# Holding the second group's cell stores and some late weights back until the first group's batch 7 has been gathered

## What is computed

```
h      = leaky_relu(bn1(conv2d(x, stem_w, stride 4)))        # 96 channels, 24 x 24
offset = conv2d(h, off_w, stride 4)                          # 2 numbers for each of 16 taps, 6 x 6 tokens
h      = leaky_relu(bn2(deform_conv(h, offset, dcn_w)))      # bilinear samples, 192 channels, 36 tokens
h      = h + attention(layernorm(h))                         # 12 heads, exp features; W_qkv, W_proj, b_proj, gamma, beta
h      = h + ffn(layernorm(h))                               # 3 experts W1, W2 chosen per image
```

## Time and profile before

| | us |
|---|---|
| median of 3 runs | 433.98 |
| lowest, highest | 433.89, 437.59 |
| the profiled execution | 433.47 |
| its span in the trace | 431.7 |
| PE busy | 375.2 |
| DVE busy | 291.9 |
| ACT busy | 218.0 |
| POOL busy | 166.8 |

### The profile page before, as it was taken

How to read it: one execution, slowest core, us unless ns; L and a number is a source line. 1 busy time by engine, 2 the same in 40 slices (tenths; PEclk the granted TensorE clock), 3 DMA queues, 4 the chain that set the end, 5 groups by cost and what they waited for, 6 DMA issues and landing times.

```text
span 431.7 us, 8223 instructions
## 1 busy us (share of the span) xinstructions
PE 375.2 (87%) x2856; PEld 274.2 (64%) x2856; DVE 291.9 (68%) x1115; ACT 218.0 (50%) x522; POOL 166.8 (39%) x168
## 2 busy tenths in 40 slices
PE   8886795888987979999889798898998978889997
PEld 4564353766783548766857486576666757757675
DVE  3854775767766877994669979555898965665222
ACT  2675754655367666435544663354455616441610
POOL 3216788780077654300666653037654200000000
PEclk9989598698999589999999999999999999999999
DMA  6679689989974523319444343015543200000000
GB/s 136 147 209 263 186 241 240 329 234 277 285 230 134 145 83 110 94 47 274 109 128 141 105 119 91 2 38 154 145 117 85 73 0 2 2 0 22 0 2 21
DMA packets 58864, 54.18 MB, mean 126 GB/s; under 512 B 42698, under 2 KB 51175, under 8 KB 58823
## 3 DMA queue, kind: packets, MB, share of 16 engines
q1 hardware_dynamic: 48968, 25.28, 23.1%
q0 software_dynamic: 9216, 28.32, 23.0%
q10 hardware_dynamic: 639, 0.05, 0.1%
HBM read 38.52 MB, written 15.11 MB: 124 GB/s over the span
## 4 chain that ended last, share of the span: by engine, by line
PE 55%; ACT 13%; DVE 13%; DMA 5%; issue 5%; POOL 5%; SPq 2%; DVEq 0%; ACTq 0%; POOLq 0%
PE bank L1172 10%; PE bank L1142 7%; PE bank L1149 5%; POOL ring L620 5%; DMA ring<-cells,cell 4%; PE bank L1076 4%; PE bank L811 4%; PE bank L723 3%; DVE bank L1725 2%; ACT hid L1570 2%; DVE o L1818 2%; PE bank L1040 2%; PE bank L685 2%; ACT bank L1343 2%; DVE acc L1725 2%
## 5 line engine op out<-in xcount | busy, mean ns | idle before, releaser
L620 POOL DMA_INDIRECT ring<-cells,cell x144 | 153.0, 1063 | 149.9 <-DVE mv L1785 69.4
L1570 ACT ACTIVATE hid<-bank,b_up 128x288 f32<-128x288 f32 x72 | 32.0, 497 | 63.6 <-PE bank L1149 63.5
L1725 DVE SCALAR_TENSOR_TENSOR acc<-ring,corner,acc 128x96 f32<-128x96 f32 x180 | 43.6, 311 | 16.7 <-ACT acc L1343 16.7
L1172 PE MATMUL bank<-w_down,hid 128*128 128x192 f32 x288 | 52.1, 332 | 0.0
L1142 PE MATMUL bank<-xfT,w_up 128*128 128x288 f32 x144 | 44.6, 433 | 5.5 <-ACT hid L1570 5.3
L1172 PEld LDWEIGHTS bank<-w_down,hid 128*128 128x128 f32 x288 | 46.2, 190 | 4.6 <-issue 4.4
L811 PE MATMUL bank<-w_dcn,shared 128*128 128x192 f32 x192 | 41.6, 356 | 6.6 <-ACT shared L1352 6.6
L1725 DVE SCALAR_TENSOR_TENSOR bank<-ring,corner,bank 128x96 f32<-128x96 f32 x168 | 39.6, 310 | 6.1 <-ACT bank L1343 6.0
L811 PEld LDWEIGHTS bank<-w_dcn,shared 128*128 128x128 f32 x192 | 33.3, 203 | 13.5 <-ACT shared L1352 9.7
L685 PE MATMUL bank<-xt,w_stem 48*96 48x384 f32 x96 | 28.5, 598 | 11.4 <-ACT h L1331 5.8
L1142 PEld LDWEIGHTS bank<-xfT,w_up 128*128 128x128 f32 x144 | 25.0, 193 | 14.7 <-ACT hid L1570 7.7
(11 more groups left out here) (207 smaller groups left out, 657.8 us busy)
## 6 DMA issues: line engine op xcount, KB each, us to landing
cells<-ring SPq DMA_DIRECT2D x12, 288.0 KB, 4.5
cells<-h SPq DMA_DIRECT2D x12, 288.0 KB, 4.6
cells<-ring SPq DMA_DIRECT2D x4, 864.0 KB, 8.0
xs<-in_x_dram SPq DMA_DIRECT2D x28, 108.0 KB
ring<-cells,cell POOLq DMA_INDIRECT x144, 3.1
cells<-w_up SPq DMA_DIRECT2D x6, 288.0 KB, 5.0
cells<-w_down SPq DMA_DIRECT2D x6, 288.0 KB, 6.9
w_down<-in_L_ffn_W_dram SPq DMA_DIRECT2D x3, 576.0 KB, 6.3
```

The source lines that it names most:

```text
L620: pool.indirect_dma_start(ring[:, ring_slot(k), j, :], None, cells[g][0:HALF_CELLS, :] if k < EARLY else cells[g], bass.IndirectOffsetOnAx ...
L1172: mm = pe.matmul(down_out(e, t), hid[:, e % 2, f, t0:t0 + n], w_down[:, e, f, :], start=(f == 0), stop=(f == FCH - 1))
L1570: act.activation(hid[:, e % 2, f, :], up_bank(g, n)[:, 0:TOK], ACT.Gelu, bias=b_up[:, n:n + 1]).then_inc(gelu_done, 1)
L1725: ins = dve.scalar_tensor_tensor(acc[:, k % 3, :, j, :] if c == 3 else part_sum, ring[:, ring_slot(k), j, C1 * c:C1 * (c + 1)].rearrange(" ...
```

## The change

SP no longer stores the first half of group 1's cells after batch 2. It issues `img`, `spread`, `w_qk`, `w_qk_rest` and `w_v`, and then waits until batch 7 of the first group's gathers has landed. Only then come the three broadcast rows (in the order `beta`, `b_proj`, `gamma`), the three transfers of `w_proj`, all twelve stores of group 1, and everything that followed them, in the old order. The six transfers held back among the weights count on a semaphore of their own, `ld_late`; `ld_attn` is waited for at 6 transfers instead of 12, and PE waits for `ld_late` at the start of `project(g)`, DVE at the start of `add_biases(g)`. No transfer and no arithmetic is added or dropped.

```diff
+        LAST_QUIET = 7
...
             for g in range(1, GROUPS):
                 store_edges(g)
-            store_half(1, 0, STORE_PARTS[1])
...
-            for dst, src in ((w_v, w["W_qkv"][:, 2 * C2:]), (w_proj, w["W_proj"])):
-                sp.dma_start(dst[:, 0, :], src[0:WIDE, :]).then_inc(ld_attn, 16)
+            def load_rows(dst, src, done):
+                sp.dma_start(dst[:, 0, :], src[0:WIDE, :]).then_inc(done, 16)
                 for i in range(2):
-                    sp.dma_start(dst[lower(i), 1, :], src[WIDE:C2, :]).then_inc(ld_attn, 16)
-            for dst, name in ((gamma, "gamma"), (beta, "beta"), (b_proj, "b_proj")):
-                sp.dma_start(dst[:, :], w[name].partition_broadcast(128)).then_inc(ld_attn, 16)
+                    sp.dma_start(dst[lower(i), 1, :], src[WIDE:C2, :]).then_inc(done, 16)
+
+            load_rows(w_v, w["W_qkv"][:, 2 * C2:], ld_attn)
+            sp.wait_ge(gathered[ring_slot(LAST_QUIET)], slot_done(0, LAST_QUIET))
+            for dst, name in ((beta, "beta"), (b_proj, "b_proj"), (gamma, "gamma")):
+                sp.dma_start(dst[:, :], w[name].partition_broadcast(128)).then_inc(ld_late, 16)
+            load_rows(w_proj, w["W_proj"], ld_late)

             def step(g, has_last, has_next):
                 if g == 0:
-                    store_half(1, 1, STORE_PARTS[1])
+                    store_cells(1)
                     load_up()
                     load_images(3, 0)
...
             def project(g):
+                pe.wait_ge(ld_late, 16 * 6)
                 pe.wait_ge(t3_evac, 3 * g + 1)
...
-                    pe.wait_ge(ld_attn, 16 * 12)
+                    pe.wait_ge(ld_attn, 16 * 6)
...
             def add_biases(g):
+                dve.wait_ge(ld_late, 16 * 6)
...
-                    dve.wait_ge(ld_attn, 16 * 12)
+                    dve.wait_ge(ld_attn, 16 * 6)
```

More of the change, by code:

```diff
@@ L261, in build @@
         w_dcn_even, w_dcn_odd, bias_evac = sem("w_dcn_even"), sem("w_dcn_odd"), sem("bias_evac")
-        ld_up, ld_down = sem("ld_up"), sem("ld_down")
+        ld_up, ld_down, ld_late = sem("ld_up"), sem("ld_down"), sem("ld_late")
         ln_chain, xn_ready = sem("ln_chain"), sem("xn_ready")
```

## The result

The changed kernel takes 446.56 us, the median of 4 runs (444.35 to 449.49); the kernel before took 435.78 on the same chip (4 runs, 433.89 to 437.69). The ratio, taken between runs made one after the other, is 1.028, interval 1.022 to 1.034. The forecast was 437.0, with a range of 431.5 to 442.0: the change is slower, by the mechanism of Rival A, but by more than three times as much as forecast (10.8 us for 3.0) and outside the range. The profiled execution of the changed kernel took 448.39 us, against 433.47 before.

A forecast was written before the change was run, and what follows sets the result against it. Gathers were taken to be on the path in the first group's sampling, where TensorE starves. Part 1's 5 us are spent waiting inside a 3.5 us loss; less 0.5 for the clock, +3.0 gives 437.0 us, range 431.5 to 442.

The forecast's parts named there:

- Rival A: PE's wait for images (3, 1) takes back the gain and more: +0.5 to +6.5 us, 434.5 to 440.5; chance 0.60.
- Part 1: Gathers of batches 4 to 7, without SP's traffic: issued and landed sooner, what follows 5 us earlier, bounds 0 and 8.
- T7: The time at which batch 7's gathers have landed and SP goes on: 84.0 us, bounds 82.9 and 88.4.
- Part 2: New waits of DVE and PE for late transfers, and of `gather(1)` for group 1's stores: hidden, costing nothing.
- Part 3: SP's queue after T7: group 1's twelve stores stand ahead of the rest, images (3, 1) ready at 143; loss 3.5 us.
- X: The time at which POOL's copies of images (3, 1) are done: 143.4 us, between 138 and 150; 143 used.
- The estimate by bytes: SP's queue and gathers after T7: 15.1 MB at 276 GB/s take 54.7 us, giving X = 142.5.
- The 464 GB/s of the forecast: Estimated rate of sixteen DMA engines: 15.1 MB would take 33 us, X = 121, and nothing would be late.
- What is late then: PE wants images (3, 1) at 132, gets them at 143, stands 11 us; `xf` transposes start at 149.8, not 146.27.
- The clock: From 137 to 150 us, part of the low clock passes while PE has no work: gain 0 to 2 us, 0.5 taken.
- The sum: Whole kernel: 3.5 - 0.5 = 3.0 us slower, 434.7 for the span, 437.0 against the median.
- Rival B: Gathers go at POOL's own pace, not slowed by SP: T7 88.4, X 147.5, time 441.5 us; chance 0.13.

The follow-up runs named there:

- narrow sums: DVE's first-group sums over 1 of 32 channels, the rest left out, in the kernel before (429.57 us) and in the changed kernel (439.16 us).
- the two kernels that stop for `w_up_rest`: Changed kernel, images (3, 0) before the wait, (3, 1) between group 2's half stores, `load_up` and `load_down` behind; wait for batch 8: 1.000, batch 7: 1.006.
- rows alone late: The kernel before with only the broadcast rows and `w_proj` held until batch 7 has landed, ahead of `load_up`; stores stay early: 437.94 us, 1.003.
- the change again: The changed kernel unaltered, timed once more on the chip of another kernel: 444.77 us, 1.018 to the kernel before.
- images (3, 1) early: The changed kernel with images (3, 1) loaded between the two halves of group 2's stores instead of after `load_down`: 437.25 us, 1.007.

## Why the prediction was wrong: a right mechanism, one step missed by 7 us

**Part 1 failed, in the step that put POOL's lateness down to SP.** The forecast allowed the stretch of batches 4 to 7 some 20.5 us in place of 23.0, on the ground that the DMA engines were full beside it. It measured 25.3, and 20.8 with narrow sums whether or not SP moved anything. The possibility that the forecast named, "the 2.83 us of the gather at 59.93 may be POOL's own", was the right one as far as SP goes, for all the long gathers; only that the cause is DVE's, and taking SP's traffic away doesn't make it smaller. T7 came at 91.0 instead of 84.0. Of these 7.0 us, 1.7 are the start of batch 4 (61.60 against 59.93, behind a gather of 4.17 us at 54.63, held already ahead of the stretch), 4.7 gathers that stood, and 0.6 the landing. The upper bound of 88.4 was also too low: it took the kernel before's own lateness as the worst, while the gathers that are held change from kernel to kernel (batches 4 to 7 took 22.6 to 25.5 us in the traces with wide sums).

**The 5 us that part 1 should have brought never came.** PE should have wanted images (3, 1) at 132 and wanted them at 140.4, later than the 137.0 before. The size was right for another cause: narrow sums alone bring PE to 131.7.

**Part 2 held.** Nothing waits for the late rows, and the first gathers of group 1 are issued at 106.7 with 122.53 still set by DVE's `mv`, as before at 119.28.

**Part 3 held, term by term.** Late weights took 3.45 us (3.6 forecast), twelve stores of group 1 13.7 (15.3), the landing 4.9 (5.7), `load_up` 6.2 (5.7), images (3, 0) 1.85, twelve stores of group 2 16.9 (15.3), `load_down` 5.8 (5.1), images (3, 1) 1.65 to issue and about 5.7 until the copy starts (4 to land), the copies 1.3. Together 61.5 us from T7 to X where 59.4 were summed: X is 152.5 instead of 143.4, 7.0 of it from T7 and 2.1 from this sum. The estimate by bytes at 276 GB/s held too: the trace has 286 GB/s from 120 to 144. The 464 GB/s of the forecast was its own estimate, sixteen times the figure for one engine; the fullest row shown is the 353 GB/s of the earlier trace rows.

**What is late then: right.** PE stood for 12.2 us (11 forecast); that the two lie so close is in part luck, since its ends were both late, by 8.4 us (140.4 for 132) and by 9.6 (152.6 for 143). It was images (3, 1) that it stood for, and from X to the transposes of `xf` it took 7.0 us (6.8). The experiment with narrow sums is this forecast with the failed term put right: SP on at 82.07, X at 143.4, `xf` at 150.37, where the text has 84.0, 143.4 and 149.8.

**The clock: wrong sign, 2.2 us.** I took 0.5 us of gain. "Rest" in the table has two values, 285.4 to 285.5 and 286.9 to 287.1, but for the two kernels that stop for `w_up_rest`. The 1.6 between the two values goes with how long the clock stays at the low level, 1.2 GHz, behind the start of `xf`: for 7.2 to 7.6 us in the four kernels with the shorter rest, for 8.5 to 9.6 us in the eight with the longer, six of which (not "rows alone late" and "the change again") show a second low stretch of 3.4 us some 15.5 us behind that start. From 8 to 20 us behind the start of `xf`, in the columns of the earlier trace rows, the kernel before has

```profile
154.27:166.27 12.00, 9.29 (x51) 7.18 (x51) 9.13 (x44) 9.99 (x27) 4.53 (x5) 1.00 0.35 98
```

and the changed one

```profile
167.48:179.48 12.00, 9.74 (x42) 7.20 (x42) 8.86 (x43) 9.48 (x26) 9.25 (x10) 0.83 0.58 156
```

The row of L817 shown above lies in the second low stretch: six products with `w_dcn` take 2.29 us at 175.60, and 1.24 at the high level. Whether the long stall causes it stays open: the kernel before with narrow sums, where PE doesn't stand before `xf`, has a rest of 286.9 as well, and images (3, 1) early has 285.5.

**The sum.** 9.5 us from X (152.5 for the 143 of the forecast), 0.2 up to `xf`, 2.2 of clock: the 11.9 us between the forecast's +3.0 and the 14.9 of the profiled pair. In the medians the miss is 7.8, since the profiled executions lie apart as said above; the change's repeat reached `xf` at 156.16.

**The chances.** Rival B was the case that came nearest, with T7 beyond its 88.4: the gathers' issue was not slowed by SP, though the pace wasn't POOL's own either. It had 0.13 and 441.5 us. The sentence against it, that no issuing engine explains a landing of 5.5 us, was sound for the landing and said nothing about the issue. One glance at DVE beside the gather of 2.83 us would have shown sums from 59.19 to 62.10, and a gather that ends 0.66 later.

## What to carry to other kernels

When transfers are held back on a queue that works in order, subtract the length of what stands behind the wait from the moment at which its last urgent transfer is wanted; here 137.0 less 60.5 to 61.6 gives 76, and batch 7 was down at 82 even with narrow sums and no traffic, so in this order no yield of the quiet could have paid for this place. Before a late issue is put down to traffic, lay the timelines of all engines beside the very instructions that were long, and look for a moment when the traffic is small: the 3.04 us at 239 us would have pointed the same way. Reordering a full queue moved the stop from one consumer to the next; before an order is given up, look whether the queue itself stands somewhere, as SP did for 15.2 us in front of a tile that wasn't free.

## What the runs showed of the hardware that I had not expected

- An indirect gather on POOL, 0.95 us by itself, took up to 4.69 us beside DVE's `scalar_tensor_tensor` of 128x96 fp32 with both tensor operands in SBUF, mostly ended 0.66 to 0.83 us after DVE's run of instructions (a few 0.29 to 0.45), and was not held by sums with one operand in PSUM nor, beyond 1.56 us, by sums of 128x3. That it is DVE's sums is shown by the two narrow kernels; that the writing of the gather's descriptors waits for DVE is not shown. The page "SBUF — State Buffer" of the Trainium skill, in its section on SBUF's two separate sides, gives that explanation for DVE's faster modes, where a DMA issued by GpSimd can't have its descriptors written; by its words a DVE instruction with two SBUF inputs should stop only a GpSimd instruction that reads SBUF. A gather of this kernel does read its cells' numbers from SBUF; no run tells the two apart.
- Quiet DMA engines shorten a gather's landing from 5.5 or 6 us to 3.0. For batches 4 to 7 alone that gave PE a net 0.3 us, in the one pair with narrow sums; with batch 8 in the quiet as well, the last products of the sampling came 3.4 to 3.8 us sooner after its last issue than in the kernel before.
- A PE that stood for 12 us came back at 1.2 GHz (0.50 granted from 150 to 164 us), and what followed the start of `xf` took one of two lengths, 1.6 us apart, which kernels with and without a stall both took.
